# The last chunk of a transformer block on one core, ended by output tiles

## The reference

```
x = x + gate_msa * attention(...)
h = layernorm(x) * (1 + scale_mlp) + shift_mlp
x = x + gate_mlp * (gelu(h @ W1 + b1) @ W2 + b2)
inv = rsqrt(mean(x * x, axis=-1) + 1e-6)
out = x * inv * rms_weight * (1 + scale) + shift
```

## Time and profile before

| | us |
|---|---|
| median of 3 runs | 4009.19 |
| lowest and highest | 4009.13, 4010.85 |
| the profiled execution | 4011.15 |
| its span, first to last instruction | 4009.4 |
| PE busy in it | 3947.7 |
| DVE, ACT and POOL busy in it | 2414.3, 1812.7, 1927.4 |

### The profile page before, as it was taken

The page is one execution under the profiler, slowest core; times in us unless marked ns, Lnnn a source line. Parts: engine busy times, 40 slices in busy tenths (PEclk is TensorE's granted clock), DMA queues, the critical chain, the costliest instruction groups (busy, mean ns, idle before and its releaser), DMA issues.

```text
span 4009.4 us, 51892 instructions
## 1 busy us (share of the span) xinstructions
PE 3947.7 (98%) x19723; PEld 2717.3 (68%) x19723; DVE 2414.3 (60%) x4020; ACT 1812.7 (45%) x3220; POOL 1927.4 (48%) x562
## 2 busy tenths in 40 slices
PE   8999999999999999999999999999999999999998
PEld 6777886445555555555555554788888888888886
DVE  3665557787878878787887875333443433344442
ACT  2222223666666666666666666333333333333332
POOL 1000004788888888887888888632112222221221
PEclk9999999999999999999999999999999999999999
DMA  5444463333233233323323332411011112111110
GB/s 197 180 180 163 185 218 94 75 70 77 59 88 75 65 76 78 79 59 88 75 65 77 78 80 64 124 35 43 35 43 35 48 40 66 43 35 43 35 43 21
DMA packets 184996, 323.72 MB, mean 81 GB/s; under 512 B 14452, under 2 KB 53428, under 8 KB 184748
## 3 DMA queue, kind: packets, MB, share of 16 engines
q1 hardware_dynamic: 184748, 320.41, 28.0%
HBM read 201.77 MB, written 117.54 MB: 80 GB/s over the span
## 4 chain that ended last, share of the span: by engine, by line
PE 93%; DVE 3%; DMA 2%; issue 1%; ACT 1%; POOL 0%; SPq 0%; POOLq 0%; ACTq 0%; DVEq 0%
PE psum L997 12%; PE psum L535 12%; PE psum L1008 12%; PE psum L436 10%; PE psum L437 10%; PE psum L438 10%; PE psum L1519 6%; PE psum L1515 6%; PE psum L1517 6%; PE psum L1024 5%; PE psum L1038 4%; DVE max_part L825 2%; PE psum L1477 1%; PE psum L471 1%; PE psum L543 0%
## 5 line engine op out<-in xcount | busy, mean ns | idle before, releaser
L825 DVE TENSOR_REDUCE max_part<-psum 128x1 f32<-128x512 f32 x2048 | 1288.6, 682 | 299.2 <-PE psum L535 292.7
L1118 ACT ACTIVATE probs<-psum 128x512 f32<-128x512 f32 x2048 | 1095.0, 599 | 619.3 <-PE psum L997 609.5
L1226 POOL TENSOR_TENSOR prob_sum<-prob_sum,probs 128x2048 f32<-128x2048 f32 x256 | 1176.8, 4597 | 29.5 <-ACT probs L1118 0.9
L535 PE MATMUL psum<-k_stack,q_stack 96*128 96x512 f32 x2048 | 771.5, 407 | 3.7 <-DVE max_part L825 1.7
L1648 DVE TENSOR_TENSOR g_parts<-g_full,g_parts 128x512 fp32r<-128x512 f32 x256 | 263.2, 1028 | 818.3 <-ACT g_parts L1557 818.3
L997 PE MATMUL psum<-q_stack,k_stack 98*128 98x512 f32 x2048 | 741.2, 408 | 4.9 <-issue 3.8
L997 PEld LDWEIGHTS psum<-q_stack,k_stack 98*128 98x128 f32 x2048 | 383.2, 190 | 247.6 <-issue 109.8
L1553 ACT ACTIVATE g_full<-psum,cols 128x512 f32<-128x512 f32 x256 | 176.6, 690 | 815.7 <-PE psum L438 815.4
L1715 POOL TENSOR_TENSOR y_out<-y_out,rows 128x512 f32<-128x512 f32 x64 | 82.9, 1296 | 936.4 <-DVE y_out L1686 936.4
L535 PEld LDWEIGHTS psum<-k_stack,q_stack 96*128 96x128 f32 x2048 | 383.3, 190 | 208.4 <-DVE max_part L825 122.8
L1008 PE MATMUL psum<-probs,v_group 128*32 128x512 f32 x4096 | 503.6, 598 | 0.0
(11 more groups left out here) (152 smaller groups left out, 4759.9 us busy)
## 6 DMA issues: line engine op xcount, KB each, us to landing
qk_parts<-qk_out SPq DMA_DIRECT2D x128, 512.0 KB, 2.8
k_stack<-qk_parts SPq DMA_DIRECT2D x96, 512.0 KB, 7.1
q_stack<-qk_parts SPq DMA_DIRECT2D x192, 256.0 KB, 9.4
x_in<-in_x SPq DMA_DIRECT2D x16, 1024.0 KB, 5.4
v_rows<-v_out SPq DMA_DIRECT2D x64, 256.0 KB, 2.0
v_group<-v_rows SPq DMA_DIRECT2D x32, 512.0 KB, 4.0
gated_attention<-gated SPq DMA_DIRECT2D x64, 256.0 KB, 4.6
x<-in_x SPq DMA_DIRECT2D x16, 1024.0 KB, 8.2
```

The source lines that it names most:

```text
L535: pe.matmul(psum[:, SMAX[at.turn % 3], :], q_stack[u % 3][0:PARTS, h, i * P:(i + 1) * P], k_stack[G % 2][0:PARTS, h, kh * CH:(kh + 1) * CH ...
L825: dve.reduce_max(max_part[:, n:n + 1], psum[:, SMAX[at.turn % 3], :], AX.X).then_inc(dve_smax, 1)
L1118: act.activation(probs[slot(u, kt)][:, h, :], psum[:, ST[n % 3], :], ACT.Exp, scale=SCALE).then_inc(act_exp, 1)
L1226: pool.tensor_tensor(total[:, :, :], total[:, :, :], probs[slot(u, kt)][:, :, :], ALU.add).then_inc(pool_sum, 1)
```

## The change

Only the end of the last chunk is written anew; chunks 0 to 14 and the up tiles of chunk 15 are as they were.

- **PE.** The down products of hidden tiles 13, 14 and 15 of the last chunk are made by pe_down_end: first tiles 13 and 14 for output tiles 0 and 1, then tile 15 for these two, then all three for output tile 2, then for output tile 3. A new semaphore pe_end counts complete output tiles.
- **DVE.** dve_end_residual makes gate and residual of one tile; dve_end_scale makes one tile's reciprocal (now of the root, one column) and the scaling, into xn_mlp. Their order is residual 0, 1, 2, scale 0, residual 3, scale 1, 2, 3.
- **ACT.** act_end first takes the root of a constant column, then for each tile the square and sum, and at once the root, with 1/D and the epsilon as scale and bias of that instruction (the epsilon column is set by POOL in chunk 1).
- **POOL and SP.** POOL adds the shift row in the four tiles of xn_mlp; SP stores each from there, with a semaphore for each tile. No step waits for a store any more, except the end of the program.

```diff
@@ -217,6 +217,8 @@
         y_out = [s3(f"y_out{i}", [P, D]) for i in range(2)]
+        rms_eps = s3("rms_eps", [P, 1])
+        rms_root = s3("rms_root", [P, TT + 1])
@@ -267,6 +269,13 @@
         dve_out, pool_out, pool_bias = sem("dve_out"), sem("pool_out"), sem("pool_bias")
+        pool_eps = sem("pool_eps")
+        pe_end, dve_end_y, dve_end_x, act_end_sq, act_end_root = (
+            sem("pe_end"), sem("dve_end_y"), sem("dve_end_x"), sem("act_end_sq"),
+            sem("act_end_root"))
+        dve_end_inv, dve_end_out, pool_end_out, a_end = (
+            sem("dve_end_inv"), sem("dve_end_out"), sem("pool_end_out"), sems("a_end", TT))
@@ -1454,7 +1463,9 @@
                     for n in range(TT):
-                        store_y(sp, c - 1, n)
+                        at = L - CH + n * P
+                        sp.wait_ge(pool_end_out, n + 1)
+                        sp.dma_start(out[B - 1, at:at + P, :], xn_mlp[:, n, :]).then_inc(a_end[n], 16)
@@ -1500,37 +1511,59 @@
             n = c * KM + i
-            gp = g_parts[n % 3]
             pe.wait_ge(act_ghi, n + 1)
...
             for m in range(TT):
-                cut = slice(m * P, (m + 1) * P)
                 if i == 0:
...
                         pe.wait_ge(dve_gated, B * KT)
-                pe.matmul(psum[:, ACC[m], :], gp[:, 0, cut], w2_hi[piece][:, at, :],
-                          start=i == 0, stop=False)
-                pe.matmul(psum[:, ACC[m], :], gp[:, 0, cut], w2_lo[piece][:, at, :],
-                          start=False, stop=False)
-                pe.matmul(psum[:, ACC[m], :], gp[:, 1, cut], w2_hi[piece][:, at, :],
-                          start=False, stop=i == KM - 1).then_inc(pe_down, 1)
+                pe_down_products(pe, n, m).then_inc(pe_down, 1)
+        def pe_down_products(pe, n, m):
+            i = n % KM
+            piece, at = divmod(i, HB)
+            gp = g_parts[n % 3]
+            cut = slice(m * P, (m + 1) * P)
+            pe.matmul(psum[:, ACC[m], :], gp[:, 0, cut], w2_hi[piece][:, at, :],
+                      start=i == 0, stop=False)
+            pe.matmul(psum[:, ACC[m], :], gp[:, 0, cut], w2_lo[piece][:, at, :],
+                      start=False, stop=False)
+            return pe.matmul(psum[:, ACC[m], :], gp[:, 1, cut], w2_hi[piece][:, at, :],
+                             start=False, stop=i == KM - 1)
+        def pe_down_end(pe):
+            n = NC * KM - 3
+            pe.wait_ge(act_ghi, n + 2)
+            pe.wait_ge(dve_glo, n + 2)
+            for m in (0, 1):
+                for k in range(2):
+                    pe_down_products(pe, n + k, m)
+            pe.wait_ge(act_ghi, n + 3)
+            pe.wait_ge(dve_glo, n + 3)
+            for m in (0, 1):
+                pe_down_products(pe, n + 2, m).then_inc(pe_end, 1)
+            for m in (2, 3):
+                for k in range(3):
+                    i = pe_down_products(pe, n + k, m)
+                i.then_inc(pe_end, 1)
         def pe_mlp(pe):
-            for c in range(NC + 1):
+            for c in range(NC):
                 for n in range(2):
-                    if 0 < c < NC:
+                    if c:
                         pe_transpose_h(pe, c, (2 * n, 2 * n + 1))
-                    if c:
                         pe_down_tile(pe, c - 1, KM - 2 + n)
-                if c < NC:
-                    for i in range(KM):
-                        pe_up_tile(pe, c, i)
-                        if i >= 2:
-                            pe_down_tile(pe, c, i - 2)
+                for i in range(KM):
+                    pe_up_tile(pe, c, i)
+                    if i >= 2 and c * KM + i < NC * KM - 1:
+                        pe_down_tile(pe, c, i - 2)
+            pe_down_end(pe)
@@ -1569,6 +1602,21 @@
+        def act_end(act):
+            act.wait_ge(pool_eps, 1)
+            act.activation(rms_root[:, TT:], rms_eps[:, :], ACT.Sqrt)
+            act.wait_ge(dve_glo, NC * KM)
+            for n in range(TT):
+                act.wait_ge(dve_end_x, n + 1)
+                if n >= 2:
+                    act.wait_ge(act_end_sq, n - 1)
+                act.activation(g_full[n % 2][:, :], x1[(NC - 1) % 2][:, n, :], ACT.Square,
+                               accum_out=square_sum[:, n:n + 1]).then_inc(act_end_sq, 1)
+                act.wait_ge(act_end_sq, n + 1)
+                act.activation(rms_root[:, n:n + 1], square_sum[:, n:n + 1], ACT.Sqrt,
+                               scale=1.0 / D, bias=rms_eps[:, :]).then_inc(act_end_root, 1)
         def act_mlp(act, done):
@@ -1590,7 +1638,7 @@
                 else:
-                    act_finish(act, c - 1)
+                    act_end(act)
@@ -1656,10 +1704,7 @@
                     dve.wait_ge(pool_bias, c + 1)
-                    if c < NC - 1:
-                        dve.wait_ge(dve_lo2, (c + 2) * KD)
-                    else:
-                        dve.wait_ge(act_sq, c * TT)
+                    dve.wait_ge(dve_lo2, (c + 2) * KD)
                 if n >= 2:
@@ -1687,12 +1732,45 @@
+        def dve_end_residual(dve, n):
+            x_tile = x1[(NC - 1) % 2][:, n, :]
+            dve.wait_ge(pe_end, n + 1)
+            if n == 0:
+                dve.wait_ge(a_r3, 64 * B)
+                dve.wait_ge(pool_bias, NC)
+                dve.wait_ge(act_sq, (NC - 1) * TT)
+            if n >= 2:
+                dve.wait_ge(dve_end_x, n - 1)
+            dve.tensor_tensor(work[n % 2][:, :], psum[:, ACC[n], :], rows3[:, 0, :],
+                              ALU.mult).then_inc(dve_end_y, 1)
+            dve.wait_ge(dve_end_y, n + 1)
+            dve.tensor_tensor(x_tile, x_tile, work[n % 2][:, :], ALU.add).then_inc(dve_end_x, 1)
+        def dve_end_scale(dve, n):
+            if n == 0:
+                dve.wait_ge(pe_tr2, NC * KD)
+            dve.wait_ge(act_end_root, n + 1)
+            dve.reciprocal(square_sum[:, n:n + 1], rms_root[:, n:n + 1]).then_inc(dve_end_inv, 1)
+            dve.wait_ge(dve_end_inv, n + 1)
+            dve.scalar_tensor_tensor(xn_mlp[:, n, :], x1[(NC - 1) % 2][:, n, :],
+                                     square_sum[:, n:n + 1], rows3[:, 2, :], ALU.mult,
+                                     ALU.mult).then_inc(dve_end_out, 1)
+        def dve_end(dve):
+            for n in range(TT):
+                dve_end_residual(dve, n)
+                if n >= 2:
+                    dve_end_scale(dve, n - 2)
+            for n in range(TT - 2, TT):
+                dve_end_scale(dve, n)
         def dve_mlp(dve):
...
                     dve_transpose_h(dve, c, (2, 3))
-                if c:
+                if 0 < c < NC:
                     dve_finish_first(dve, c - 1)
@@ -1704,9 +1782,7 @@
                 else:
-                    dve_finish_second(dve, c - 1)
-                    for n in range(TT):
-                        dve_finish_third(dve, c - 1, n)
+                    dve_end(dve)
@@ -1728,6 +1804,9 @@
                             pool_finish_third(pool, c - 1, i - 3)
+                        if c == 1 and i == 0:
+                            pool.memset(rms_eps[:, :], RMS_EPS).then_inc(pool_eps, 1)
                         if i == 10 and c + 1 < NC:
@@ -1739,7 +1818,9 @@
                     for n in range(TT):
-                        pool_finish_third(pool, c - 1, n)
+                        pool.wait_ge(dve_end_out, n + 1)
+                        pool.tensor_tensor(xn_mlp[:, n, :], xn_mlp[:, n, :], rows3[:, 3, :],
+                                           ALU.add).then_inc(pool_end_out, 1)
@@ -1752,7 +1833,9 @@
             for k in range(2):
-                sp.wait_ge(a_y[k], 16 * (NC * TT // 2))
+                sp.wait_ge(a_y[k], 16 * ((NC - 1) * TT // 2))
+            for n in range(TT):
+                sp.wait_ge(a_end[n], 16)
```

## The result

| | before | changed |
|---|---|---|
| median, first timing (20 runs each) | 4011.12 | 4002.34 |
| lowest to highest | 4008.74 to 4014.62 | 4001.14 to 4008.90 |
| the profiled span | 4009.4 | 4000.1 |

The ratio of the runs is 0.998, with a 95% interval of 0.9974 to 0.9987; the medians themselves are 0.22% apart, 8.8 us. The forecast was 7.9 us, 0.198%, called "within 0.2%" with the larger chance. The time lies in the range given. The interval leaves out 1, so there is a gain, but it runs from 0.13% to 0.26% and holds both 0.198% and 0.22%. The medians fell on the other side of the bound that the forecast stood on; the means of the same runs, 4011.33 and 4003.47, are 7.9 us apart, on the forecast's side. The two profiled spans differ by 9.3 us. So two things have to be found out: whether the sum was right, and where the further 0.8 to 1.3 us come from.

A forecast was written before the change was run, and what follows sets the result against it. The chain was 93% PE, untouched; only the end could change, at most 27 us. Earlier DVE start, table load off the path, no store waits and DVE-POOL turns gave 7.94 us less: 4001.3 us, range 3999.4 to 4003.0.

The forecast's parts named there:

- the bound that the forecast stood on: The 0.2% limit for telling a change from none: 8.0 us, or 4001.2 us; the forecast lay just inside.
- What bounds the end, and what stays: End of the last chunk: at most 27 us alterable; products stay 0.233 us apart, final store and closing stay 2.53 us.
- PE's order: Last 36 products: same count reordered, no stall with 0.6 us cover; DVE begins at 3985.94 rather than 3988.74.
- ACT: End of last chunk: the table load's 1.28 us leave the path; 128x1 Sqrt 0.21, upper end 0.63, without moving the sum.
- Turns of DVE and POOL: Last four tiles: add 3, scalings and POOL additions exclude each other, 1.89 us per tile; last addition 7.94 us earlier.
- Rival 1: DVE, not POOL, wins the turn at scaling 2, by a 0.05 us margin; another 0.2 us, 4001.0; chance 0.2.
- Rival 2: No turns between DVE and POOL at the end, additions follow without gaps: 3999.4 us; chance 0.05.
- 3 (a second table load): ACT's Square and Sqrt don't share tables, two loads per tile: gain only 3.0, 4006.2 us; chance 0.02.
- 4 (late stores): Last stores from one four-tile buffer land late, up to 10.3 us: 4009.6, slower than before; chance 0.02.
- Sum: Whole kernel: 4011.15 less 7.94 gives 4003.2; the run median is 1.96 lower, so 4001.3, or -0.198%.
- How the numbers follow: Chances and range: forecast 0.6, split 0.27 beyond and 0.33 within; faster 0.46, within 0.2% 0.51, slower 0.03; 3999.4 to 4003.0.

The follow-up runs named there:

- no_add: Changed kernel without POOL's four shift-row additions in the last chunk; from PE's last product start to the last operation's end 4.51 us, against 8.48.
- turn: Changed kernel with reciprocals 1 and 2 made together ahead of scalings 1 and 2; from PE's last product start to the last operation's end 8.02 us, against 8.48.
- pe_only: Changed kernel's product order, with the other engines' old end; from PE's last product start to the last operation's end 14.56 us, against 16.46 before.
- pe_old: Changed kernel with the old order of PE's products; from PE's last product start to the last operation's end 11.12 us, against 16.46 before.
- four_buf: Kernel before, with the last chunk's results in four tiles, no store waits; from PE's last product start to the last operation's end 14.96 us, against 16.46.
- dve_add: Changed kernel with the four shift-row additions on DVE, POOL idle; from PE's last product start to the last operation's end 6.76 us, against 8.48.
- again: Changed kernel, unaltered, timed a second time: median 4002.71 us against 4012.28 for the kernel before, ratio 0.9977.
- fold_pool: Changed kernel with x times weight row made before the root, tiles 1 and 2 on POOL, then one DVE operation: 4001.45 us, ratio 0.9977.

## Why the prediction came out as it did

- **What bounds the end, and what stays.** Right: the products kept 0.233 us, the closing took 2.55 us where before it took 2.49.
- **PE's order.** Right: first multiply 4.47 us before the last product's start, as forecast (3985.94 to 3990.41 and 3984.57 to 3989.04); no stall.
- **ACT.** Right on the path. The 128x1 Sqrt took 0.30, between the 0.21 taken and the 0.63 of the upper end; the 128x1 reciprocal 0.15 for 0.18. Neither moved the end.
- **Turns of DVE and POOL.** Right, and the term that mattered: add 3 1.25 (forecast 1.26), scalings 2 and 3 1.78 (1.76), POOL first at scaling 2, by 0.03 for the forecast's 0.05. no_add shows what the sum would have missed without it. Rival 1's mechanism is real, as turn shows, but did not occur in the three profiles of the changed kernel; in turn, where a reciprocal moved with it, the end came 0.46 earlier, not 0.2. Rival 2 (no turns), 3 (a second table load) and 4 (late stores) are out: add 3 and two scalings were held up, there was one load, and the last store landed 2.04 us after its issue.
- **Sum.** The stretch shrank by 7.98, against 7.94 in the forecast. That is the mechanism and not luck: pe_only, pe_old, four_buf, no_add and turn each took the time that the same turns and waits gave them, to 0.1 us.
- **How the numbers follow: here it failed.** Two steps. The first is "so 4001.3, or -0.198% ... just inside" and the split "0.27 beyond and 0.33 within" built on it: a sum with an error of a few hundredths of a us was read as if the medians followed it to 0.01%. The three timings put the same 8.0 us at 0.22%, 0.24% and 0.19% by their medians, and the kernel timed against itself has an interval of 0.999 to 1.0008, which is 3 to 4 us on each side. With a sum right on the bound, which side a timing shows is decided by where PE arrives in its executions (within the profiles of one kernel nothing else varies by 0.1 us) and by the 1.7 to 3.0 us that a time is longer than its span, and the larger chance for "within" had no ground. Such an interval tells 8 us from none, but not 7.9 from 8.0, nor the further 0.8 us of the first timing (0.02%) from nothing: that they are spread is the likelier reading, and stays open. The second is "the runs before spread by 1.7 us, the odd one above", from three runs. With 20 runs the spread of the kernel before is 5.9 us and its median 4011.12, 1.9 above the 4009.19 that the forecast was set on. On that median the sum of 7.94 gives 4003.2, just outside the range of 3999.4 to 4003.0. The time of 4002.34 fell inside because the level was 1.9 too low and the gap of the medians 0.8 larger than the sum: luck, not a level that was known. (The chances listed for the forecast, the rivals and the rest add up to 0.99, not 1.)

## What to carry to other kernels

When steps that stood in a row are interleaved by tile, sum them with the turns that DVE and POOL take: a DVE operation with two SBUF inputs that starts beside a POOL addition ends 0.55 us after it, one that reads PSUM kept its 0.68 to 0.69, and the turn of 1.89 us per tile was dearer than the same work on DVE alone, 1.39 in dve_add, with POOL left idle. A wait that is removed is worth only what the next constraint leaves of it: the same four buffers brought 1.50 us in one order and 0.44 in the other. For an edit at the end of a long program, compare the stretch from a common event in the profile; it repeated to 0.01 us where the whole time moved by several. And where a sum lies on a bound that the timing can't resolve, say that either side is as likely.

## What the runs showed of the hardware that was not expected

- PE's last product started anywhere from 3986.79 to 3994.02 us in 14 profiles of programs that are one up to there. Most of the difference between turn and no_add comes in the first 120 us, where the mean granted clock of the 14 is 0.89 to 0.96, and some from 2500 to 2600 us. In again, four_buf and fold_pool another 1.7 to 2.1 us against turn come between 120 and 700 us.
- Who waits in a turn matters. With POOL ahead a tile takes 1.89 us; with both waiting for each other in alternation, as in four_buf and turn, POOL's additions of 1.70 start every 1.67 us.
